# Full attention with 16-channel heads: row-maximum products in whole sets of four, started in another row group, and the projected keys, queries and values read out of PSUM by ScalarE

## The chip, the cores and the metric

The kernel runs on one core of one Trainium2 chip. The metric is the device time of one execution in microseconds (us). The change touches one of the six stages of the kernel, the second layer's cross attention, which takes about 1,240 us of the 8,617 us.

## The reference, cut to what matters

The whole kernel is a decoder of two layers on x of shape (4, 512, 256). The stage in question computes, for each of 4 batches, with 16 heads of 16 channels, over 1,601 context positions:

```
q = _split_heads(Q @ W_q.T + b_q)
k = _split_heads(K @ W_k.T + b_k)
v = _split_heads(V @ W_v.T + b_v)
scores = jnp.einsum('bhqd,bhkd->bhqk', q, k) / jnp.sqrt(jnp.float32(D_K))
probs = jax.nn.softmax(scores, axis=-1)
ctx = jnp.einsum('bhqk,bhkd->bhqd', probs, v)
...
return ctx @ W_o.T + b_o
```

Q is the layer-normalised x; K and V are both the context.

## The kernel before

A head of 16 channels is padded to 32 rows, so four heads (j = 0 to 3) fill the 128 rows of TensorE (PE), each in its own row group of 32. A **unit** is one batch and one group of four heads: 4 batches by 4 groups, 16 units. All matrix data is 32-bit.

For softmax a unit needs the largest score of every row before the exponentials. The scores are therefore computed twice:

- **Chunks** (maximum products): 64 per unit, one for each head j, query tile t of 128 and key block n of 400 or 401 columns. `chunk` on PE writes a bank of a ring of three PSUM banks (`fa_ring`, L1845); VectorE (DVE) reduces it to one maximum per row (L1753). `row_max`, `turn_less` and `shift` then fold the negated maximum into the queries `Qm`.
- **Scores** proper (L1866): keys by rows, 128 by 512 for each j, into four banks `fa_sps` of their own; ScalarE (ACT) takes the exponential of each (L1715); `output` multiplies with the values into `fa_pv` (L1877).

A unit has 13 **slots**, one for each 128 keys. In slot s PE issues the scores of slot s + 1, and between them chunks of the next unit (so the chunks of unit u + 1 run beside the scores of unit u), then what stands below, then `output` of slot s. 64 chunks are spread over slots 0 to 10: 5 or 6 in each. Chunk i has head `i % FJ`, so the head with which a slot's chunks begin changes from slot to slot: slots 0 to 10 begin with heads 0, 1, 3, 1, 3, 1, 2, 0, 2, 0, 2. The scores always begin with head 0.

**Pieces** are the projections of keys, queries and values of the next batch: 33 in each batch (4 of Q, 16 of K, of which 4 have only 65 columns, 13 of V). They go through the same ring. They are issued one in a slot in the units of groups 1, 2 and 3 of the first three batches (all 13 slots of groups 1 and 2, slots 0 to 6 of group 3); group 0 has none, and batch 3 has none. The first batch's pieces stand ahead of unit 0, with unit 0's chunks between them. DVE adds the bias while it copies a piece out (L1741 V, L1744 Q, L1747 K).

In slot 1 PE issues `add_up` (the sums of the softmax, into the ring) and DVE takes the reciprocal (L1770) and scales (L1772). In slots 4 and 5 of a new batch `out_product` follows for the batch before.

Every engine works its own list in order. All users of the ring take turns in one order written out by hand (`turn`); PE waits before a turn until the user three turns earlier has been read out (`await_bank`), and one semaphore, `ring_free`, counts every read-out, since DVE does them all. The core of PE's loop:

```python
for j in range(FJ):
    if nxt and nxt != (u + 1, 0):
        scores(*nxt, j)
    if j < len(ahead):
        chunk(u + 1, ahead[j])
for i in ahead[FJ:]:
    chunk(u + 1, i)
...
output(u, slot)
```

Of the kernel before, what the change touches and what calls it, by code (L numbers as in the profile page):

```python
# [1554 lines left out]
def lay_full_attention(a, rows, cols):  # L1555
# [10 lines left out]
    for j in range(FJ):  # L1566
# [4 lines left out]
        "fa_wv": rows(g("W_v").T), "fa_bv": g("b_v"),  # L1571
# [5 lines left out]
def full_attention(nc, c):  # L1577
# [7 lines left out]
    CHUNKS = FJ * TB * NKB  # L1585
# [3 lines left out]
    with Scope(nc, "fa") as s:  # L1589
# [4 lines left out]
        bv = s.sb("bv", [P, D])  # L1594
# [24 lines left out]
        ring_free = s.sem("ring_free")  # L1619
        top_ready = s.sem("top_ready")  # L1620
# [40 lines left out]
        turn = {}  # L1661

        def take(*use):
            turn[use] = len(turn)

        for n in range(len(PIECES)):
            take("piece", 0, n)
            for i in first_chunks(n - FIRST) if n >= FIRST else ():
                take("chunk", 0, i)
        take("less", 0)  # L1670
        for u, (b, g) in enumerate(UNITS):
            for slot in range(KT):
                for i in chunks_of(slot) if u < LAST_UNIT else ():
                    take("chunk", u + 1, i)
                if slot == LESS_SLOT and u < LAST_UNIT:
                    take("less", u + 1)
                if piece_of(u, slot) is not None:
                    take("piece", b + 1, piece_of(u, slot))
                if slot == SUMS_SLOT and u:
                    take("sums", u - 1)  # L1680
# [10 lines left out]
        def _(sp):  # L1691
            for dst, src in ((wq, "wq"), (wk, "wk"), (bqk, "bqk"), (wv, "wv"), (wo, "wo"), (sums, "sums")):
                sp.dma_start(dst[:], c.dram[f"fa_{src}"]).then_inc(loaded, 16)
            for dst, src in ((bv, "bv"), (bo, "bo")):
                sp.dma_start(dst[:], c.dram[f"fa_{src}"].partition_broadcast(P)).then_inc(loaded, 16)
# [6 lines left out]
        def _(pool):  # L1702
            nc.gpsimd.memset(less[:], 0.0).then_inc(made, 1)
            nc.gpsimd.memset(V[:, :, :, :, FD:], 1.0).then_inc(made, 1)
            pool.wait_ge(loaded, LOADS)
            nc.gpsimd.tensor_tensor(c.x[:], c.x[:], bo[:].unsqueeze(1).broadcast_to([P, NT, D]), ALU.add).then_inc(based, 1)

        @block.scalar
        def _(act):
# [6 lines left out]

            def take_output(u):
# [5 lines left out]
            for u in range(len(UNITS)):  # L1723
                for kt in range(KT):
                    exps(u, kt)
                    if kt == 0 and u:
                        take_output(u - 1)
            take_output(LAST_UNIT)

        @block.vector  # L1730
        def _(dve):
            def await_turn(*use):
                dve.wait_ge(ring_ready, turn[use] + 1)

            def piece(b, n):
                what, g, m = PIECES[n]
                await_turn("piece", b, n)
                src = bank("piece", b, n)
                if what == "V":
                    rows = keys(m)  # L1740
                    ins = nc.vector.tensor_tensor(V[0:rows, b % 2, m, :, 0:FD], src[0:rows, 0:D].rearrange("p (h d) -> p h d", d=FD),  # L1741
                                                  bv[0:rows, :].rearrange("p (h d) -> p h d", d=FD), ALU.add)
                elif what == "Q":
                    ins = nc.vector.tensor_scalar(Q[:, b % 2, g, :], src[:], bqk[:, 0, g:g + 1], None, ALU.add)  # L1744
                else:
                    k0, w = KEYS[m]
                    ins = nc.vector.tensor_scalar(K[:, b % 2, g, k0:k0 + w], src[:, 0:w], bqk[:, 1, g:g + 1], None, ALU.add)  # L1747
                ins.then_inc(ring_free, 1)
# [7 lines left out]
            def row_max(u):  # L1756
                dve.wait_ge(ring_free, turn["chunk", u, CHUNKS - 1] + 1)
# [5 lines left out]
            def shift(u):  # L1763
                b, g = UNITS[u]
                await_turn("less", u)
                nc.vector.tensor_tensor(Qm[:, u % 2, :], bank("less", u)[:], Q[:, b % 2, g, :], ALU.add).then_inc(ring_free, 1)

            def scale(u):
                await_turn("sums", u)
                nc.vector.reciprocal(share[:], bank("sums", u)[:]).then_inc(ring_free, 1)  # L1770
                dve.wait_ge(ring_free, turn["sums", u] + 1)
# [11 lines left out]
            for n in range(len(PIECES)):  # L1783
                piece(0, n)
                for i in first_chunks(n - FIRST) if n >= FIRST else ():
                    chunk(0, i)
# [3 lines left out]
            for u, (b, g) in enumerate(UNITS):  # L1790
                for slot in range(KT):
                    if u < LAST_UNIT:
                        for i in chunks_of(slot):
                            chunk(u + 1, i)
                        if slot == MAX_SLOTS - 1:
                            row_max(u + 1)
                        if slot == LESS_SLOT:
                            shift(u + 1)
                    if piece_of(u, slot) is not None:
                        piece(b + 1, piece_of(u, slot))  # L1800
# [9 lines left out]
        def _(pe):  # L1810
            def await_bank(*use):

                if turn[use] >= RING:
                    pe.wait_ge(ring_free, turn[use] - RING + 1)
# [21 lines left out]
            def chunk(u, i):  # L1836
# [4 lines left out]
                if i == 0:  # L1841
                    pe.wait_ge(ring_free, turn["piece", b, PIECES.index(("K", g, len(KEYS) - 1))] + 1)
# [13 lines left out]
            def scores(u, kt, j):  # L1856
# [4 lines left out]
                if kt == 0 and j == 0:  # L1861
                    pe.wait_ge(ring_free, turn["less", u] + 1)
# [6 lines left out]
            def output(u, kt):  # L1869

                b, g = UNITS[u]
                n = keys(kt)
                if kt == 0 and u:
# [25 lines left out]
            pe.wait_ge(made, MADE)  # L1899
            for n in range(len(PIECES)):  # L1900
# [1241 lines left out]
```

## Time and profile before

| | |
|---|---|
| median of 3 runs | 8619.73 us (8613.97 to 8625.38) |
| the profiled execution's own time | 8617.03 us |
| its span, first to last instruction | 8615.2 us |
| mean granted TensorE clock | 0.913 |
| the stage: first piece to last `out_product` | about 6720 to 7955 us of the span |
| PE, DVE, ACT busy over the whole span | 83%, 56%, 33% |

PE is the matmul stream and PEld the weight loads beside it. A 32-bit matmul shows as two instructions. In a timeline row the columns are the start, the length, the engine and line, the operation, what is written and read, how many instructions are merged, and in brackets the idle time before them with what ended it. "PEclk" is the clock that was granted, 1.00 being 2.4 GHz and 0.50 being 1.2 GHz.

### The profile page before, as it was taken

The numbers are of one execution on the slowest core, as the hardware profiler recorded it, in microseconds if no ns is written. First come the engines' busy times: TensorE is split into PE (matmuls) and PEld (weight loads), VectorE is DVE, ScalarE is ACT, GpSimd is POOL, SyncE is SP. The second block draws the span as 40 slices with busy tenths as digits, with TensorE's granted clock in tenths as the row PEclk, the third lists the DMA queues.
The fourth block names the chain that finished last, engine by engine and source line by source line (L and its number), as shares of the span: only waits on it lengthen the run. The fifth ranks groups of instructions, "written<-read, shape, count | busy, mean of one in ns | idle before, by whom it ended". The sixth has DMA issues, their size and how long they took to land. (4 is left out here: it accounts for less than half of the span.)

```text
span 8615.2 us, 102487 instructions
## 1 busy us (share of the span) xinstructions
PE 7109.9 (83%) x35402; PEld 4802.5 (56%) x35402; DVE 4861.0 (56%) x7898; ACT 2854.5 (33%) x5165; POOL 711.7 (8%) x695
## 2 busy tenths in 40 slices
PE   6887887887879888888888889956653899999799
PEld 4775766756757666666666744422222334333577
DVE  5656655656646666666666610058886555555621
ACT  3223222232224444444444411134441233334210
POOL 0111111111100000000000000023333000000000
PEclk8998998998989999999999999978886899999895
DMA  0000000000000000000000010000000000000110
GB/s 33 0 1 1 0 1 1 0 1 1 0 33 9 7 20 9 7 20 7 8 19 9 7 55 0 0 18 0 0 0 3 26 8 1 8 1 1 40 49 10
DMA packets 23873, 89.02 MB, mean 10 GB/s; under 512 B 5784, under 2 KB 9120, under 8 KB 18480
## 3 DMA queue, kind: packets, MB, share of 16 engines
q1 hardware_dynamic: 23456, 83.53, 2.8%
q8 instruction: 253, 4.15, 0.2%
q14 instruction: 164, 1.34, 0.1%
HBM read 81.43 MB, written 2.10 MB: 10 GB/s over the span
## 5 line engine op out<-in xcount | busy, mean ns | idle before, releaser
L1252 DVE TENSOR_TENSOR xa_PT<-xa_tps,xa_PT 128x512 fp32r<-128x512 f32 (+1 forms) x1024 | 555.3, 584 | 386.0 <-ACT xa_PT L1127 382.3
L1753 DVE TENSOR_REDUCE fa_part<-fa_ring 128x1 f32<-128x400 f32 (+1 forms) x1024 | 533.0, 569 | 330.2 <-PE fa_ring L1845 312.3
L1715 ACT ACTIVATE fa_prob<-fa_sps 128x512 f32<-128x512 f32 (+1 forms) x832 | 439.9, 601 | 782.8 <-PE fa_sps L1866 774.1
L635 DVE TENSOR_TENSOR gdn_XX<-gdn_XX,gdn_wps 128x512 f32<-128x512 f32 (+1 forms) x768 | 477.2, 640 | 367.8 <-PE gdn_wps L799 360.1
L496 ACT ACTIVATE gdn_Y<-gdn_yps 128x256 f32<-128x256 f32 x768 | 295.2, 384 | 1051.6 <-PE gdn_yps L784 1045.2
L1405 PE MATMUL xa_tps<-ident,xa_prob 128*128 128x128 f32 (+1 forms) x3328 | 501.4, 284 | 162.3 <-DVE xa_PT L1252 161.6
L1845 PE MATMUL fa_ring<-fa_K,fa_Q 32*128 32x400 f32 (+1 forms) x2048 | 586.6, 546 | 36.7 <-DVE fa_part L1753 23.5
L1405 PEld LDWEIGHTS xa_tps<-ident,xa_prob 128*128 128x128 f32 (+1 forms) x3328 | 393.1, 143 | 388.6 <-DVE xa_PT L1252 317.7
L1127 ACT ACTIVATE xa_PT<-xa_tps 128x512 fp32r<-128x512 f32 (+1 forms) x1024 | 471.2, 514 | 416.1 <-PE xa_tps L1405 415.9
L796 PE MATMUL gdn_wps<-gdn_Y,gdn_XX 128*128 128x128 f32 x3072 | 601.2, 287 | 2.9
L1240 DVE CUSTOM_DVE_ANT_0 xa_prob<-xa_sps,xa_mask 128x1604 f32<-128x1604 f32 x256 | 467.4, 1826 | 130.0 <-PE xa_sps L1387 123.4
L796 PEld LDWEIGHTS gdn_wps<-gdn_Y,gdn_XX 128*128 128x128 f32 x3072 | 472.9, 196 | 67.4 <-issue 35.9
L1115 ACT ACTIVATE xa_prob<-xa_prob,xa_neg 128x1604 f32<-128x1604 f32 x256 | 418.2, 1634 | 268.2 <-DVE xa_neg L1243 268.1
L799 PE MATMUL gdn_wps<-gdn_XX,gdn_Y 128*128 128x128 f32 x2560 | 503.5, 279 | 0.0
L1387 PE MATMUL xa_sps<-xa_K,xa_Q 128*128 128x402 f32 x2048 | 466.7, 372 | 29.6 <-issue 16.9
L1423 PE MATMUL xa_pv<-xa_PT,xa_V 128*128 128x256 f32 (+1 forms) x3328 | 453.4, 292 | 11.1 <-DVE xa_PT L1252 11.1
L2042 PE MATMUL ffn_mid<-ffn_hid,ffn_h 128*128 128x512 f32 x1024 | 441.5, 593 | 9.7 <-DVE ffn_hid L2008 6.3
L1423 PEld LDWEIGHTS xa_pv<-xa_PT,xa_V 128*128 128x128 f32 (+1 forms) x3328 | 415.9, 189 | 49.2 <-issue 28.8
L2361 DVE TENSOR_TENSOR_SCAN scan_h<-scan_dA,scan_dBx 128x2048 f32<-128x2048 f32 x64 | 407.8, 6372 | 26.4 <-POOL scan_dBx L2235 20.2
L1387 PEld LDWEIGHTS xa_sps<-xa_K,xa_Q 128*128 128x128 f32 x2048 | 382.7, 198 | 45.1 <-issue 36.0
L799 PEld LDWEIGHTS gdn_wps<-gdn_XX,gdn_Y 128*128 128x128 f32 x2560 | 398.5, 196 | 0.0
L1845 PEld LDWEIGHTS fa_ring<-fa_K,fa_Q 32*128 32x128 f32 x2048 | 245.9, 187 | 270.9 <-DVE fa_part L1753 222.2
(424 smaller groups left out, 12365.8 us busy)
## 6 DMA issues: line engine op xcount, KB each, us to landing
xa_wqk<-in_xa_wqk SPq DMA_DIRECT2D x64, 256.0 KB, 2.6
moe_own_w<-in_moe_w SPq DMA_DIRECT2D x14, 1024.0 KB
ffn_h<-in_ffn_h SPq DMA_DIRECT2D x2, 4096.0 KB, 27.5
xa_ctxT<-in_ctxT SPq DMA_DIRECT2D x4, 1601.0 KB
fa_ctxT<-in_ctxT SPq DMA_DIRECT2D x4, 1601.0 KB
xa_mask<-in_mask SPq DMA_DIRECT2D x4, 802.0 KB, 9.0
ffn_w<-in_ffn_w SPq DMA_DIRECT2D x3, 1024.0 KB, 18.1
x<-in_x SPq DMA_DIRECT2D x1, 2048.0 KB
```

The lines of the kernel that those rows point to most:

```text
L635: nc.vector.tensor_tensor(X[:, half, 0:n], X[:, half, 0:n], wps[half][:, 0:n], ALU.subtract).then_inc(X_ready, 1)
L796: last = nc.tensor.matmul(wps[half][:, 0, e, :], X[:, half, 1, e, :], Y[:, h, :], start=True, stop=True)
L799: last = nc.tensor.matmul(wps[half][:, 1, e, :], Y[:, h, :], X[:, half, 1, e, :], start=True, stop=True)
L1127: nc.scalar.activation(PT[0:n, u // 2 % NPT, 0, k0:k1, u % 2, :], turned_bank(u, g)[0:n, 0:k1 - k0, :], ACT.Copy).then_inc(t_hi, 1)
L1240: nc.vector.tensor_tensor_reduce(parts(prob[:, e, :]), sps[:, :, 0:SW], parts(mask[:, u % TB if masked else 0, :]), 1.0, -3.0e38, ALU.add, ...
L1252: nc.vector.tensor_tensor(PT[0:n, u // 2 % NPT, 1, k0:k1, u % 2, :], turned_bank(u, g)[0:n, 0:k1 - k0, :], PT[0:n, u // 2 % NPT, 0, k0:k1, ...
L1387: last = nc.tensor.matmul(sps[:, n, 0:SWW], Q[:, hh % 2, e, q * P:(q + 1) * P], k, start=(e == 0), stop=(e == 1))
L1405: last = nc.tensor.transpose(turned_bank(u, g)[0:n, kt - k0, :], prob[:, u % 2, kt * P:kt * P + n], c.ident[:])
L1423: nc.tensor.matmul(pv[0:MV, 0:2 * P], V[0:n, kt, hh].rearrange("p e d -> p (e d)"), PT[0:n, pair % NPT, part, kt].rearrange("p a q -> p (a ...
L1753: nc.vector.tensor_reduce(part[:, t, j, n:n + 1], bank("chunk", u, i)[:, 0:KB[n][1]], AX, ALU.max).then_inc(ring_free, 1)
L1845: nc.tensor.matmul(bank("chunk", u, i)[:, 0:w], Q[rows, b % 2, g, t * P:(t + 1) * P], K[rows, b % 2, g, k0:k0 + w], start=True, stop=True) ...
L2042: last = nc.tensor.matmul(mid[m % 2][:], w[n][:, k, m * P:(m + 1) * P], hid[e][:, k, :], start=(k == 0), stop=(k == MH - 1))
```

## The change

1. Chunks are dealt out in sets of four (`QUADS`, 16 to a unit): every slot from 0 to 10 has one set between the scores (`early`), and slots 2, 4, 6, 8 and 10 have a second one (`late`). `chunk_at` shifts the head by two, so every set begins with head 2 while the scores begin with head 0.
2. A late set comes after the slot's piece and before `output`. In slots without a late set `output` moves ahead of `add_up` and of `out_product`.
3. Pieces are read out by ScalarE (`piece` under `block.scalar`), in its list after the exponentials of the slot and before those of the next; a second semaphore, `piece_taken`, counts them, and `await_bank` picks the semaphore by who had the bank (`nth`).
4. ScalarE can't add a bias along the row to V, so the bias of V is folded into that of the output: GpSimd spreads it (`bv_wide`), PE multiplies it with the output weights into a first turn of the ring (`base`, eight matmul instructions of 256 columns) before the first piece, DVE adds that to `bo`, and GpSimd's addition of `bo` to x waits for it.

```diff
-            return range(CHUNKS * min(slot, MAX_SLOTS) // MAX_SLOTS, CHUNKS * min(slot + 1, MAX_SLOTS) // MAX_SLOTS)
+            first, last = (QUADS * min(n, MAX_SLOTS) // MAX_SLOTS * FJ for n in (slot, slot + 1))
+            return range(first, min(first + FJ, last)), range(first + FJ, last)
...
-            return i % FJ, i // FJ // NKB, i // FJ % NKB
+            return (i + FJ // 2) % FJ, i // FJ // NKB, i // FJ % NKB
...
+            nc.gpsimd.tensor_copy(bv_wide[:], bv[:].unsqueeze(2).broadcast_to([P, FG, P])).then_inc(spread_ready, 1)
+            pool.wait_ge(ring_free, nth["base",])
             nc.gpsimd.tensor_tensor(c.x[:], c.x[:], bo[:].unsqueeze(1).broadcast_to([P, NT, D]), ALU.add).then_inc(based, 1)
...
+            def piece(b, n):
+                what, g, m = PIECES[n]
+                act.wait_ge(ring_ready, turn["piece", b, n] + 1)
+                src = bank("piece", b, n)
+                if what == "V":
+                    rows = keys(m)
+                    ins = nc.scalar.activation(V[0:rows, b % 2, m, :, 0:FD], src[0:rows, 0:D].rearrange("p (h d) -> p h d", d=FD), ACT.Copy)
+                elif what == "Q":
+                    ins = nc.scalar.activation(Q[:, b % 2, g, :], src[:], ACT.Identity, bias=bqk[:, 0, g:g + 1])
+                else:
+                    k0, w = KEYS[m]
+                    ins = nc.scalar.activation(K[:, b % 2, g, k0:k0 + w], src[:, 0:w], ACT.Identity, bias=bqk[:, 1, g:g + 1])
+                ins.then_inc(piece_taken, 1)
...
                 for kt in range(KT):
                     exps(u, kt)
                     if kt == 0 and u:
                         take_output(u - 1)
+                    if piece_of(u, kt) is not None:
+                        piece(b + 1, piece_of(u, kt))
...
             def await_bank(*use):
 
                 if turn[use] >= RING:
-                    pe.wait_ge(ring_free, turn[use] - RING + 1)
+                    before = uses[turn[use] - RING]
+                    pe.wait_ge(piece_taken if before[0] == "piece" else ring_free, nth[before])
...
+            pe.wait_ge(spread_ready, 1)
+            for g in range(FG):
+                last = nc.tensor.matmul(bank("base")[:, 0:D], bv_wide[:, g, :], wo[:, g, :], start=(g == 0), stop=(g == FG - 1))
+            last.then_inc(ring_ready, 1)
...
                     for j in range(FJ):
-                        if nxt and nxt != (u + 1, 0):
-                            scores(*nxt, j)
-                        if j < len(ahead):
-                            chunk(u + 1, ahead[j])
-                    for i in ahead[FJ:]:
-                        chunk(u + 1, i)
+                        if slot + 1 < KT:
+                            scores(u, slot + 1, j)
+                        if j < len(early):
+                            chunk(u + 1, early[j])
                     if slot == LESS_SLOT and u < LAST_UNIT:
                         turn_less(u + 1)
                     if piece_of(u, slot) is not None:
                         piece(b + 1, piece_of(u, slot))
-                    if nxt == (u + 1, 0):
+                    if slot + 1 == KT and u < LAST_UNIT:
                         for j in range(FJ):
-                            scores(*nxt, j)
+                            scores(u + 1, 0, j)
+                    if not late:
+                        output(u, slot)
+                    for i in late:
+                        chunk(u + 1, i)
                     if slot == SUMS_SLOT and u:
                         add_up(u - 1)
                     if slot in OUT_SLOTS and u and ends(u - 1):
                         out_product(b - 1, OUT_SLOTS.index(slot))
-                    output(u, slot)
+                    if late:
+                        output(u, slot)
```

## Rows read from the trace of the kernel before

**Rows 1.** Busy time (instructions) of PE, PEld, DVE, ACT, POOL, then PEclk: units 0 and 14.

```profile
6804.00:6866.00 62.00, 59.81 (x332) 23.82 (x328) 34.18 (x67) 26.45 (x51) 0.00 (x0) 0.90 0.01 4
...
7836.00:7902.00 66.00, 63.25 (x348) 23.45 (x344) 38.65 (x70) 28.44 (x55) 0.00 (x0) 0.92 0.00 1
```

**Rows 2.** Timeline of ACT in unit 0, the exponentials of slots 3 to 12.

```profile
6821.80 2.06 ACT L1715 ACTIVATE fa_prob<-fa_sps 128x512 f32<-128x512 f32 x4 [2.58 <-PE fa_sps L1866]
6826.59 2.26 ACT L1715 ACTIVATE fa_prob<-fa_sps 128x512 f32<-128x512 f32 x4 [2.72 <-PE fa_sps L1866]
...
6840.57 2.06 ACT L1715 ACTIVATE fa_prob<-fa_sps 128x512 f32<-128x512 f32 x4 [2.10 <-PE fa_sps L1866]
6845.21 2.29 ACT L1715 ACTIVATE fa_prob<-fa_sps 128x512 f32<-128x512 f32 x4 [2.58 <-PE fa_sps L1866]
6850.48 2.06 ACT L1715 ACTIVATE fa_prob<-fa_sps 128x512 f32<-128x512 f32 x4 [2.98 <-PE fa_sps L1866]
...
6864.98 2.05 ACT L1715 ACTIVATE fa_prob<-fa_sps 65x512 f32<-65x512 f32 x4 [2.52 <-PE fa_sps L1866]
```

**Rows 3.** Timeline of one slot with six chunks, and the next one's start.

```profile
7809.27 0.18 PEld L1866 LDWEIGHTS fa_sps<-fa_Qm,fa_K 32*128 32x128 f32 x1 [0.85 <-issue]
...
7810.47 3.14 DVE L1753 TENSOR_REDUCE fa_part<-fa_ring 128x1 f32<-128x401 f32 x6 [1.50 <-PE fa_ring L1845]
...
7811.10 0.29 PEld L1845 LDWEIGHTS fa_ring<-fa_K,fa_Q 32*128 32x128 f32 x2 [0.68 <-DVE fa_part L1753]
...
7812.06 0.29 PEld L1845 LDWEIGHTS fa_ring<-fa_K,fa_Q 32*128 32x128 f32 x2 [0.19 <-DVE fa_part L1753]
7812.93 0.13 PEld L1877 LDWEIGHTS fa_pv<-fa_prob,fa_V 128*17 128x17 f32 x8 [0.57 <-ACT fa_prob L1715]
...
7813.91 0.33 PEld L1866 LDWEIGHTS fa_sps<-fa_Qm,fa_K 32*128 32x128 f32 x8 [0.85 <-issue]
...
7815.74 3.14 DVE L1753 TENSOR_REDUCE fa_part<-fa_ring 128x1 f32<-128x400 f32 x6 [2.13 <-PE fa_ring L1845]
```

**Rows 4.** Timeline of ACT, slots 0 and 1 of the fifth unit.

```profile
7105.78 2.29 ACT L1715 ACTIVATE fa_prob<-fa_sps 128x512 f32<-128x512 f32 x4
...
7116.47 1.57 ACT L1715 ACTIVATE fa_prob<-fa_sps 128x512 f32<-128x512 f32 x3 [3.64 <-PE fa_sps L1866]
```

**Rows 5.** Timeline around the reciprocal, with a piece of Q after the chunks.

```profile
7045.27 3.36 DVE L1770 RECIPROCAL fa_share<-fa_ring 128x512 f32<-128x512 f32 x1 [0.63 <-PE fa_ring L1885]
...
7046.14 0.18 PEld L1866 LDWEIGHTS fa_sps<-fa_Qm,fa_K 32*128 32x128 f32 x1 [0.85 <-issue]
...
7048.68 0.18 PEld L1845 LDWEIGHTS fa_ring<-fa_K,fa_Q 32*128 32x128 f32 x1 [1.39 <-DVE fa_share L1770]
...
7049.89 0.29 PEld L1845 LDWEIGHTS fa_ring<-fa_K,fa_Q 32*128 32x128 f32 x2 [0.91 <-DVE fa_part L1753]
...
7051.72 0.30 PEld L1828 LDWEIGHTS fa_ring<-xnT,fa_wq 128*128 128x128 f32 x2 [0.57 <-DVE fa_part L1753]
...
7053.63 0.13 PEld L1877 LDWEIGHTS fa_pv<-fa_prob,fa_V 128*17 128x17 f32 x8 [0.76 <-issue]
```

**Rows 6.** Waits in the stage: total us, times, longest us.

```profile
PEld fa_sps L1866 <- ACT fa_prob L1715: 28.7, 48, 2.2
```

**Rows 7.** Groups by line on ACT: line, shapes, count, busy us, mean ns, idle.

```profile
L496 ACT ACTIVATE gdn_Y<-gdn_yps 128x256 f32<-128x256 f32 x768 | 295.2, 384 | 1051.6 <-PE gdn_yps L784 1045.2
...
L1105 ACT ACTIVATE xa_Q<-xa_proj,xa_bqk 128x512 fp32r<-128x512 f32 x64 | 43.8, 685 | 51.7 <-PE xa_proj L1369 51.6
```

**Rows 8.** Timeline of the start of the stage.

```profile
6716.12 8.82 POOL L1706 TENSOR_TENSOR x<-x,fa_bo 128x4096 f32<-128x4096 f32 x1 [7.82 <-DMA fa_bo<-in_fa_bo]
...
6720.05 3.75 PE L1828 MATMUL fa_ring<-xnT,fa_wq 128*128 128x512 f32 x4 [14.87 <-DMA fa_ctxT<-in_ctxT]
...
6724.44 0.34 PEld L1832 LDWEIGHTS fa_ring<-fa_ctxT,fa_wk 128*128 128x128 f32 x1 [0.52 <-issue]
6725.02 0.19 PEld L1832 LDWEIGHTS fa_ring<-fa_ctxT,fa_wk 128*128 128x128 f32 x1 [0.24 <-issue]
```

More of the change, by code:

```diff
@@ L1659, in ends @@
             return UNITS[u][1] == FG - 1
-        turn = {}
+        turn, uses, nth = {}, [], {}
+        counts = {True: 0, False: 0}
         def take(*use):
             turn[use] = len(turn)
+            uses.append(use)
+            counts[use[0] == "piece"] += 1
+            nth[use] = counts[use[0] == "piece"]
+        take("base")
         for n in range(len(PIECES)):
@@ L1672, in full_attention @@
             for slot in range(KT):
-                for i in chunks_of(slot) if u < LAST_UNIT else ():
+                early, late = chunks_of(slot) if u < LAST_UNIT else ((), ())
+                for i in early:
                     take("chunk", u + 1, i)
@@ L1678, in full_attention @@
                     take("piece", b + 1, piece_of(u, slot))
+                for i in late:
+                    take("chunk", u + 1, i)
                 if slot == SUMS_SLOT and u:
@@ L1721, in take_output @@
                 nc.scalar.activation(raw[:], pv[:], ACT.Copy).then_inc(raw_ready, 1)
-            for u in range(len(UNITS)):
+            act.wait_ge(loaded, LOADS)
+            act.wait_ge(made, MADE)
+            for n in range(len(PIECES)):
+                piece(0, n)
+            for u, (b, g) in enumerate(UNITS):
                 for kt in range(KT):
@@ L1782, in _ @@
             dve.wait_ge(made, MADE)
[L1783 to L1786, printed above, removed]
+            dve.wait_ge(ring_ready, turn["base",] + 1)
+            nc.vector.tensor_tensor(bo[:], bank("base")[:, 0:D], bo[:], ALU.add).then_inc(ring_free, 1)
+            for i in range(CHUNKS):
+                chunk(0, i)
             row_max(0)
@@ L1791, in _ @@
                 for slot in range(KT):
-                    if u < LAST_UNIT:
-                        for i in chunks_of(slot):
-                            chunk(u + 1, i)
[L1795 to L1800, printed above, removed]
+                    early, late = chunks_of(slot) if u < LAST_UNIT else ((), ())
+                    for i in early:
+                        chunk(u + 1, i)
+                    if slot == LESS_SLOT and u < LAST_UNIT:
+                        shift(u + 1)
+                    for i in late:
+                        chunk(u + 1, i)
+                    if slot == MAX_SLOTS - 1 and u < LAST_UNIT:
+                        row_max(u + 1)
                     if slot == SUMS_SLOT and u:
@@ L1841, in chunk @@
                 if i == 0:
-                    pe.wait_ge(ring_free, turn["piece", b, PIECES.index(("K", g, len(KEYS) - 1))] + 1)
+                    pe.wait_ge(piece_taken, nth["piece", b, PIECES.index(("K", g, len(KEYS) - 1))])
                 await_bank("chunk", u, i)
@@ L1861, in scores @@
                 if kt == 0 and j == 0:
-                    pe.wait_ge(ring_free, turn["less", u] + 1)
+                    pe.wait_ge(ring_free, nth["less", u])
                 if at >= FJ:
@@ L1872, in output @@
                 n = keys(kt)
+                if kt == 0 and g == 0:
+                    pe.wait_ge(piece_taken, nth["piece", b, PIECES.index(("V", 0, KT - 1))])
                 if kt == 0 and u:
```

40 lines of the change are left out of this document (15 added, 25 removed).

## The prediction

> **What bounds the stage now.** I read the busy times by window first, one window to a unit [rows 1]. PE is busy for 96% of every unit (59.81 of 62, 63.25 of 66), DVE for 55 to 60%, ACT for some 43% in these two; nothing is loaded from outside that anyone waits for. So the stage goes at the pace of PE's list, and PE's list is in order: what counts is how long each slot holds it.
>
> Next, ACT's timeline, because each slot's exponentials start 1.16 us after PE starts the slot's scores, so they mark the slots [rows 2]. Slots 3 to 10 of unit 0 take 6864.98 - 6826.59 = 38.39 us together. With six chunks a slot that begins with head 3 takes 6826.59 - 6821.80 = 4.79, one with head 2 takes 6845.21 - 6840.57 = 4.64, and one with head 0, the head with which the scores begin too, 6850.48 - 6845.21 = 5.27.
>
> Then one slot from inside [rows 3]. Counted from its first score at 7809.27: first reduce +1.20, weights of the fourth chunk +1.83, of the sixth +2.79, `output` +3.66, next slot +4.64. The fourth chunk waits for the first one's bank, and so on: a chunk is reduced 0.98 after its weights start (7812.06 against the last of six reduces, 7810.47 + 3.14 - 0.57), and its bank is free 0.57 + 0.06 later, so three chunks turn round in 1.61, some 0.5 each. After the last chunk's weights PE needs 0.87 until it can go on, and `output` takes 0.98. In the slot that begins with head 0 the first reduce comes 7815.74 - 7813.91 = 1.83 after the start, not 1.20.
>
> **Part 1, sets of four from head 2.** A slot with one set: the fourth chunk's weights at +1.83, +0.87 = 2.70, `output` 0.98: 3.68 us. A slot with two sets and no piece: fourth chunk reduced at +2.81, so the seventh starts at +3.44 and the eighth, likewise, at +3.92; +0.87 + 0.98 = 5.77. The eleven slots before, without the sums: slots 0 and 1 take 7116.47 - 7105.78 = 10.69 [rows 4], of which `add_up` is 1.06 (an `output` is moved, not lengthened, by it), slot 2 is 4.79, slots 3 to 10 are 38.39: 52.81. After: 6 x 3.68 + 5 x 5.77 = 50.93. That is 1.9 us a unit, nearly all of it from the three slots that began with head 0 (3 x 0.63). The number of chunks is the same, and a set that is cut off early only brings the next slot forward.
>
> The row already shows the new pairing, since slots 6, 8 and 10 begin with head 2: their first reduce still comes at +1.20, 0.04 after the first exponential. By the Trainium skill (TensorE: Matmul & The Clock Gate, "What overlaps and what doesn't") matmuls end strictly in program order, so a chunk issued behind a score can't end ahead of it, in whatever row group. The trace agrees by that +1.20; if it were not so, the first reduce could come near +0.98, and the eleven sets of fifteen units would save 0.22 each, 36 us more.
>
> **Part 2, `output` ahead of `add_up`.** Before, the reciprocal starts at 7045.27, while PE is in `output`, and slot 2 begins at 7046.14. The third chunk needs the bank of the sums and waits until 7048.68 (+2.54), with the fourth score behind it; the fourth starts at +3.75, PE goes on at 7051.72 (+5.58), and with `output` slot 2 holds PE for 6.56 [rows 5]. After, `add_up` is the last thing of slot 1, so the reciprocal starts 0.10 after slot 2 begins: third chunk at 0.10 + 3.36 + 0.02 = +3.48; DVE scales until +4.15, so the fourth starts at +4.78, the seventh at +6.39, the eighth at +6.87; + 0.87 + 0.98 = 8.72. With slot 1 at 3.68 + 1.06 = 4.74 the unit's eleven slots are 5 x 3.68 + 4.74 + 8.72 + 4 x 5.77 = 54.94, against 10.69 + 6.56 + 38.39 = 55.64 before. So of the 1.9 gained, 1.2 goes back: 0.7 is left. Sum of the units with chunks beside them: unit 0 (no sums) -1.9, the other fourteen -0.7 each: **-11.7 us**.
>
> **Part 3, pieces by ScalarE.** What DVE gives up (0.42 for a V, 0.75 for a Q or K) lies in its idle time before the slot's first reduce, so it is worth nothing. What ACT takes on is small too: nearest rows 0.38 for 128x256 and 0.69 for 128x512 with a bias [rows 7], 99 pieces in the steady part, ACT at 43% at most. What matters is its place in ACT's list: the exponentials of the next slot now wait for the piece. Let P be the end of the piece's matmuls. In a slot with one set PE does `output` and is at the next scores at P + 0.98. ACT ends the piece at P + 0.5 (V) or P + 0.85 (Q, K) and its four exponentials (0.49 apart) free the score banks at P + 1.16 to 2.63, or 1.45 to 2.90. PE's list has each score between chunks, so the last score starts some 1.7 or 1.95 into the slot where the fourth chunk would start at 1.83 anyway. I take 0.1 us for V (and the 65-column K) and 0.3 for Q and K; bounds are 0 (the fourth chunk hides it) and the whole piece, 0.38 and 0.69. Slot 1 is covered by `add_up`. There are 7 wide and 6 narrow such slots in a batch: 2.7 us; slot 12 of group 1 another 0.3.
>
> In a slot with two sets the piece now cuts the run of eight. The second set finds two banks free at P; its third chunk has the piece's bank, read out at P + 0.55 to 0.85; its fourth waits for the first: 0.98 + 0.57 + 0.06 = P + 1.61, and PE goes on at P + 2.48. Uncut it would be 4.79 + piece - (2.70 + piece) = 2.09 for these four. So 0.39 for each of 13 such slots: 5.1 us a batch. Bounds: 0 and 0.7. The pieces themselves cost PE what they did, 7053.63 - 7051.72 = 1.91 for a Q or K [rows 5]. Over three batches: 3 x (2.7 + 0.3 + 5.1) = **+24.3 us**.
>
> **Part 4, the bias.** The first piece waits for the context until 6720.05. `bo` has landed by 6716.12; GpSimd spreads 512 elements (an eighth of 8.82, 1.1 us), so `base` starts near 6717.3 and its eight instructions of 256 columns at half clock take some 3.4 us, to 6720.8: 0.7 late. But PE runs at half clock from 6720.0 to about 6725.0 (weight loads 0.34, then 0.19) [rows 8], and if those five microseconds at half clock start 2.7 us earlier, 1.35 comes back. In the rest of the startup PE's list sets the pace and DVE's share is hidden. **-0.5 us**, bounds -2 and +1. The later addition of `bo` to x on GpSimd has 80 us to end in.
>
> **Clock.** The granted clock is 0.90 to 1.00 in the units. A unit loses (1 - clock) x its length, from 6.2 us (unit 0) and 5.3 (unit 14) [rows 1] to 0 in the four units of group 3; summed over fifteen such windows 34 us. In several the low clock follows the stall behind the reciprocal, during which PE has nothing for 1.5 us. That stall is now 1 us longer and comes in every unit, so I expect a low stretch (1.6 us) where there was none or less: **+8 us**, bounds -34 (all gone) and +25.
>
> **Sum.** -11.7 + 24.3 - 0.5 + 8 = +20.1. The profiled execution took 8617.0, so 8637; the median of the runs is 2.7 above it: 8640 us.
>
> **Rivals.**
> - *Faster: the clock holds.* The slots with one set are 3.68 us with no DVE wait beyond the fourth chunk, so PE's work is denser between stalls. If the low stretches disappear, -34 takes the place of +8: 8620 - 11.7 + 24.3 - 0.5 - 34 = 8598. It decides from -30 on, so nearly all must go. Against it: PE's longest stall grows.
> - *Faster: read-out by two engines.* PE's weight loads wait for DVE before the fourth and later chunks of every slot. If DVE's pace, not the turn-round of three banks, set these waits, taking 52 x 0.42, 16 x 0.75 and 64 x 0.64 us from it would show: up to 22 + 12 + 41 = 75 us in all, and at three fifths of that 8620 + 20 - 45 = 8595. Against it: those read-outs fall where DVE is idle. The Trainium skill (TensorEngine Tiling (Array Packing), "PSUM Bottleneck") says to read PSUM out with both engines once tiling has sped up the matmuls. By that rule the change would gain; the rows say DVE has room.
> - *No measurable change.* The waits for exponentials are hidden and the clock stays as it is: -11.7 + 3 x 5.1 (the cut runs only) = +3.6, 8623; with the 8 of the clock, 8632.
> - *Clearly slower: ACT becomes the chain.* In a run of slots with one set or two, piece, four exponentials, scores and the next piece hang on each other: 0.1 + 0.69 + 2.07 + 0.05 + 1.0 + 1.91 = 5.8 against 2.70 + 1.91 + 0.98 = 5.6 for a slot with one set and a K. If each of the 99 pieces costs its upper bound (48 x 0.69 + 51 x 0.38 = 52.5 us for the 24.3 counted) the time is 8640 + 28 = 8668. It decides from 0.5 us a piece.
>
> **Chances.** My own sum 45%, its own range 8628 to 8658; no measurable change 23%; the clock holds 10%; two engines 10%; ACT as the chain 12%. A difference of 0.2% (17 us) is what a measurement of this kernel can tell from none. My sum is only just beyond it: about a fifth of that case falls inside, most of "no change" too. Together: faster 20%, within 0.2% 32%, slower 48%. For the range I take in both outer cases to their prices but leave their far sides: 8598 to 8670.
>
> **What the profile after would show.** Slots with one set and no piece 3.7 us apart, with two 5.8; first reduce +1.20 in all of them; the reciprocal starting with slot 2's first score and that slot at 8.7; exponentials after a piece starting at P + 0.5 to 0.9 and PE's weight loads of scores waiting for ACT more than the 28.7 us of before [rows 6]; the second set after a piece 2.5 long; no unit at clock 1.00. Wrong would be: second sets that run at more than two chunks at once, which would make the order pay, or units of batch 3, which have no pieces, that differ by more than 1 us from before.

## The result, and the profile after

| | before | after |
|---|---|---|
| median | 8619.93 us (5 runs, 8613.97 to 8626.68) | 8668.87 us (5 runs, 8660.9 to 8674.14) |
| profiled execution, its span | 8617.03, 8615.2 us | 8673.85, 8672.1 us |
| the stage, between the two table loads that bracket it | 1265.8 us | 1314.8 us |

The ratio is 1.0055, 95% interval 1.0041 to 1.007: slower by 49 us where 20 were forecast. In the profiled executions the stage grew by 49.0 us; the other 8 us between the two lie ahead of it, in code that is the same.

Inside the stage, measured from one `fa_raw` to the next, the part ahead of unit 0 is 1.7 us shorter, unit 0 is 1.7 longer, units 1 to 14 are 50.0 longer, and unit 15 with the tail is 1.1 shorter. To see what the clock took I add up (1 - clock) x length over the fifteen lengths that begin at the first `fa_raw`, which are units 1 to 15: 27.3 us before and 74.1 after. I call this sum the loss. Unit 0 stands outside it and loses 6.2 us before (62 x 0.10) and 10.9 after (64 x 0.17).

The windows of after that answer [rows 1], with a batch 3 unit behind them (columns as there):

```profile
6811.00:6875.00 64.00, 63.16 (x332) 25.07 (x328) 34.54 (x67) 26.24 (x51) 0.00 (x0) 0.83 0.01 2
7825.00:7893.00 68.00, 66.13 (x343) 26.05 (x342) 38.59 (x69) 27.49 (x53) 0.00 (x0) 0.85 0.00 1
7893.00:7962.00 69.00, 67.12 (x350) 26.55 (x344) 38.59 (x69) 27.74 (x55) 0.00 (x0) 0.85 0.00 1
```

DVE and ACT have as much room as before; what fell is the clock, from 0.90 and 0.92 to 0.83 and 0.85, in units that have no pieces at all. ACT's timeline in the unit at 7825, the exponentials of slots 5 to 12, shows where:

```profile
7852.33 2.06 ACT L1729 ACTIVATE fa_prob<-fa_sps 128x512 f32<-128x512 f32 x4 [1.48 <-PE fa_sps L1887]
7859.53 2.07 ACT L1729 ACTIVATE fa_prob<-fa_sps 128x512 f32<-128x512 f32 x4 [5.13 <-PE fa_sps L1887]
7863.21 2.06 ACT L1729 ACTIVATE fa_prob<-fa_sps 128x512 f32<-128x512 f32 x4 [1.61 <-PE fa_sps L1887]
7870.57 2.06 ACT L1729 ACTIVATE fa_prob<-fa_sps 128x512 f32<-128x512 f32 x4 [5.29 <-PE fa_sps L1887]
7874.25 2.06 ACT L1729 ACTIVATE fa_prob<-fa_sps 128x512 f32<-128x512 f32 x4 [1.61 <-PE fa_sps L1887]
7880.01 2.06 ACT L1729 ACTIVATE fa_prob<-fa_sps 128x512 f32<-128x512 f32 x4 [3.70 <-PE fa_sps L1887]
7883.69 2.06 ACT L1729 ACTIVATE fa_prob<-fa_sps 128x512 f32<-128x512 f32 x4 [1.61 <-PE fa_sps L1887]
7890.99 2.05 ACT L1729 ACTIVATE fa_prob<-fa_sps 65x512 f32<-65x512 f32 x4 [5.24 <-PE fa_sps L1887]
```

Slots with one set take 3.68 us (7863.21 - 7859.53), as forecast. Of the four with two sets one takes the forecast 5.76 (7880.01 - 7874.25), the other three 7.20, 7.36 and 7.30. The windows of 2 us over the second of the long ones:

```profile
7862.00:7864.00 2.00, 1.98 (x19) 1.06 (x16) 0.74 (x2) 0.79 (x2) 0.00 (x0) 1.00 0.00 0
7864.00:7866.00 2.00, 2.00 (x9) 1.08 (x9) 1.94 (x5) 1.28 (x3) 0.00 (x0) 1.00 0.00 0
7866.00:7868.00 2.00, 2.00 (x12) 0.42 (x10) 1.55 (x3) 0.00 (x0) 0.00 (x0) 0.65 0.00 0
7868.00:7870.00 2.00, 2.00 (x16) 0.84 (x11) 0.00 (x0) 0.00 (x0) 0.00 (x0) 0.50 0.00 0
7870.00:7872.00 2.00, 1.97 (x14) 0.79 (x8) 1.39 (x3) 1.43 (x3) 0.00 (x0) 0.99 0.00 0
```

and rows of its timeline:

```profile
7863.26 4.42 DVE L1772 TENSOR_REDUCE fa_part<-fa_ring 128x1 f32<-128x401 f32 x8 [1.50 <-PE fa_ring L1866]
...
7864.37 0.29 PEld L1866 LDWEIGHTS fa_ring<-fa_K,fa_Q 32*128 32x128 f32 x2 [0.19 <-DVE fa_part L1772]
...
7865.49 0.29 PEld L1866 LDWEIGHTS fa_ring<-fa_K,fa_Q 32*128 32x128 f32 x2 [0.35 <-DVE fa_part L1772]
7865.97 0.29 PEld L1866 LDWEIGHTS fa_ring<-fa_K,fa_Q 32*128 32x128 f32 x2 [0.19 <-DVE fa_part L1772]
7867.00 0.15 PEld L1900 LDWEIGHTS fa_pv<-fa_prob,fa_V 128*17 128x17 f32 x8 [0.74 <-issue]
7867.00 1.91 PE L1900 MATMUL fa_pv<-fa_prob,fa_V 128*17 128x512 f32 x8
7868.84 0.28 PEld L1887 LDWEIGHTS fa_sps<-fa_Qm,fa_K 32*128 32x128 f32 x1 [1.69 <-issue]
```

Eight reduces run without a gap (4.42 us); PE, at full clock, starts each chunk from the fourth on when a bank comes free. Behind the eighth the clock is 1.2 GHz for some 3 us: `output` holds PE 1.84 instead of 0.98, the scores behind it the rest. The slot is 7.36 - 5.76 = 1.60 longer, and by (1 - clock) x length the three windows lose 0.70 + 1.00 + 0.02 = 1.72: a lost microsecond is 0.93 us of time here.

The reciprocal, after, which answers [rows 5]:

```profile
7835.42 3.36 DVE L1790 RECIPROCAL fa_share<-fa_ring 128x512 f32<-128x512 f32 x1 [1.47 <-PE fa_ring L1908]
...
7838.83 0.18 PEld L1866 LDWEIGHTS fa_ring<-fa_K,fa_Q 32*128 32x128 f32 x1 [2.55 <-DVE fa_share L1790]
...
7840.05 1.45 PEld L1866 LDWEIGHTS fa_ring<-fa_K,fa_Q 32*128 32x128 f32 x6 [0.91 <-DVE fa_part L1772]
...
7844.52 1.91 PE L1900 MATMUL fa_pv<-fa_prob,fa_V 128*17 128x512 f32 x8
...
7846.36 0.28 PEld L1887 LDWEIGHTS fa_sps<-fa_Qm,fa_K 32*128 32x128 f32 x1 [1.69 <-issue]
```

Slot 2 begins at 7835.32; the third chunk starts at +3.51 (forecast 3.48), the fourth at +4.73 (4.78). The rest was to end at 8.72 and ends at 11.04, its `output` at half clock. This is where most of the new loss stands. The table gives the loss of units 1 to 14 in slots 2 and 3, beside and behind the reciprocal, and in slots 4 to 10, each slot taken from its first weight load of `fa_sps` to that of the next; the last two rows are experiments described below.

| | slots 2 and 3 | slots 4 to 10 |
|---|---|---|
| before | 20.5 us | 8.5 us |
| after | 57.3 | 16.0 |
| `sums_first` (the shorter stall of before, runs of eight as after) | 22.2 | 16.2 |
| `set_after_output` (the longer stall as after, no run of eight) | 54.6 | 0.0 |

These sums take the clock as it is and not rounded to 0.01, so they add up to 1 or 2 us more than the 27.3 and 74.1. Of the rise, 37 us stand in slots 2 and 3, and 35 of them go again when only the longer stall is taken back; 7.5 net stand in slots 4 to 10. Slot 2 of unit 5 in these four kernels, in this order:

```profile
7188.77:7197.24 8.47, 7.64 (x36) 2.67 (x32) 6.91 (x9) 2.17 (x4) 0.00 (x0) 1.00 0.00 0
7206.86:7220.93 14.07, 12.11 (x37) 4.00 (x36) 8.18 (x10) 3.35 (x7) 0.00 (x0) 0.76 0.00 0
7194.75:7204.73 9.98, 9.16 (x40) 2.96 (x36) 7.31 (x10) 3.54 (x7) 0.00 (x0) 1.00 0.00 0
7193.33:7206.56 13.23, 10.85 (x36) 3.12 (x35) 6.70 (x8) 3.34 (x7) 0.00 (x0) 0.74 0.00 0
```

ACT's groups, which answer [rows 7], and two rows of the waits in the stage, the first of which answers [rows 6]:

```profile
L1742 ACT ACTIVATE fa_K<-fa_ring,fa_bqk 128x512 f32<-128x512 f32 x64 | 38.0, 595 | 214.2 <-PE fa_ring L1853 214.2
L1737 ACT ACTIVATE fa_V<-fa_ring 128x256 f32<-128x256 f32 (+1 forms) x52 | 20.0, 385 | 166.8 <-PE fa_ring L1846 166.8
L1739 ACT ACTIVATE fa_Q<-fa_ring,fa_bqk 128x512 f32<-128x512 f32 x16 | 11.0, 687 | 91.3 <-PE fa_ring L1849 91.3
```

```profile
PEld fa_sps L1887 <- ACT fa_prob L1729: 139.3, 263, 2.2
...
PEld fa_ring L1866 <- DVE fa_share L1790: 35.7, 14, 2.6
```

Reading a piece takes what [rows 7] said, 385 and 687 ns. PE's wait for exponentials rose from 28.7 us in 48 waits to 139.3 in 263, but most of that is probably time in which it would have waited for a bank next: its waits for `fa_part` before chunks fell from 213 to 152 us, and `sets_only`, which has only 56 us of these waits, is no faster. The cut second set behind a V, from its first weights to `output`:

```profile
6937.19 0.30 PEld L1866 LDWEIGHTS fa_ring<-fa_K,fa_Q 32*128 32x128 f32 x4 [0.33 <-DVE fa_part L1772]
...
6938.80 0.29 PEld L1866 LDWEIGHTS fa_ring<-fa_K,fa_Q 32*128 32x128 f32 x2 [0.77 <-DVE fa_part L1772]
6939.66 0.13 PEld L1900 LDWEIGHTS fa_pv<-fa_prob,fa_V 128*17 128x17 f32 x8 [0.57 <-ACT fa_prob L1729]
```

2.47 us, the fourth chunk at +1.61, as forecast (2.48, 1.61). And the start of the stage, which answers [rows 8]:

```profile
6725.28 3.75 PE L1925 MATMUL fa_ring<-fa_wo,fa_bv_wide 128*128 128x256 f32 x8 [11.45 <-POOL fa_bv_wide L1718]
6728.41 0.75 PEld L1849 LDWEIGHTS fa_ring<-xnT,fa_wq 128*128 128x128 f32 x2
...
6730.26 0.19 PEld L1849 LDWEIGHTS fa_ring<-xnT,fa_wq 128*128 128x128 f32 x1 [0.24 <-issue]
```

The stage starts 8.67 us later in this execution, so before's first piece would stand at 6728.72; here it has its weights at 6728.41, and the half clock is over at 6730.26 instead of 6733.69 (6725.02 + 8.67).

### The profile page after: what moved, and what is told of

Read it like the earlier page. It is cut to its first block and busy times, and to the rows that moved or that the text cites. A ratio compares the mean times of both kernels' runs of the same rounds, so it can differ in the third digit from the quotient of the medians.

```text
span 8672.1 us, 102523 instructions
## 1 busy us (share of the span) xinstructions
PE 7164.7 (83%) x35410; PEld 4828.1 (56%) x35410; DVE 4794.8 (55%) x7767; ACT 2903.1 (33%) x5297; POOL 711.3 (8%) x696
## 5 line engine op out<-in xcount | busy, mean ns | idle before, releaser
L1866 PE MATMUL fa_ring<-fa_K,fa_Q 32*128 32x400 f32 (+1 forms) x2048 | 691.1, 579 | 30.5 <-DVE fa_share L1790 24.1
L1887 PE MATMUL fa_sps<-fa_Qm,fa_K 32*128 32x512 f32 (+1 forms) x1664 | 436.7, 664 | 7.4 <-ACT fa_prob L1729 6.6
L2390 DVE TENSOR_TENSOR_SCAN scan_h<-scan_dA,scan_dBx 128x2048 f32<-128x2048 f32 x64 | 407.6, 6370 | 26.4 <-POOL scan_dBx L2264 20.2
L1866 PEld LDWEIGHTS fa_ring<-fa_K,fa_Q 32*128 32x128 f32 x2048 | 274.7, 196 | 239.3 <-DVE fa_part L1772 161.4
```

Source lines behind the costliest of these rows:

```text
L1866: nc.tensor.matmul(bank("chunk", u, i)[:, 0:w], Q[rows, b % 2, g, t * P:(t + 1) * P], K[rows, b % 2, g, k0:k0 + w], start=True, stop=True) ...
```

## The experiments

Theory A, formed on these rows: a long run of chunks paced by the banks, and the longer stall at the reciprocal, lower the clock, and that is what the forecast lacked. Rival B: the read-out by ScalarE costs more than counted and is the loss. Each result is a median with its ratio to before and that ratio's 95% interval; the loss is that of the one profiled execution, so a time and a loss can come from different executions.

**One part at a time.** `sets_only` is the kernel after with `piece` moved back from ScalarE's list to VectorE's.

```diff
-                ins = nc.scalar.activation(Q[:, b % 2, g, :], src[:], ACT.Identity, bias=bqk[:, 0, g:g + 1])
+                ins = nc.vector.tensor_scalar(Q[:, b % 2, g, :], src[:], bqk[:, 0, g:g + 1], None, ALU.add)
```

> The changed kernel with the pieces read out by VectorE again (the order of PE's list, the sets of four and the bias product stay). In the changed kernel unit windows lose some 85 us to a granted clock under 1.00, against 34 before, and the low stretches stand behind the runs of eight chunks. Theory A (the runs of eight lower the clock, ScalarE is nearly innocent): the waits for exponentials after a piece go (9 us), the rest stays, so about 8655 us, and the low stretches in the units without pieces stay where they are. Rival B (pieces on ScalarE are the cost): most of the 49 us goes, about 8620 us.

Measured: 8673.25, ratio 1.0059 [1.0047, 1.0071], loss 97.6. Parts 1, 2 and 4 by themselves cost 52 us where -12.2 were counted. Rival B falls. Theory A's 8655 was missed too, by 18 us: it did not expect the loss to rise, and it is 23.5 us over after's. The rise is mostly in slots 4 to 10 (34.8 against 16.0). In the six units in which every slot has a piece, so that a piece stands between the two sets, after loses nothing there; `sets_only` loses 12.0, in slots 4 and 5 of three of them, and why is not known.

`act_only` is the kernel after with before's dealing and `output` last.

```diff
-            first, last = (QUADS * min(n, MAX_SLOTS) // MAX_SLOTS * FJ for n in (slot, slot + 1))
-            return range(first, min(first + FJ, last)), range(first + FJ, last)
+            return range(CHUNKS * min(slot, MAX_SLOTS) // MAX_SLOTS, CHUNKS * min(slot + 1, MAX_SLOTS) // MAX_SLOTS), ()
...
-            return (i + FJ // 2) % FJ, i // FJ // NKB, i // FJ % NKB
+            return i % FJ, i // FJ // NKB, i // FJ % NKB
```

> The changed kernel with the chunks dealt out as before (5 or 6 in a slot, beginning with changing heads) and output last in each slot, so only the read-out by ScalarE and the bias product are new. Theory A: no run of eight, so the clock is as before; what is left is the wait for exponentials behind a piece, up to 0.3 us for 33 pieces in three batches, 8625 to 8645 us. Rival B: 8660 us or more.

Measured: 8635.48, ratio 1.0016 [1.0007, 1.0024], loss 25.0. ScalarE's read-out, with the bias product, costs 14 us (6 to 21 by the interval) and leaves the clock alone. Beside sets it costs nothing on balance (after is 4 us under `sets_only`, within what the two intervals allow), because there the loss is 23.5 us smaller with it.

**Where `output` stands.** `sums_first` is the kernel after with `output` last in every slot.

```diff
-                    if not late:
-                        output(u, slot)
...
-                    if late:
-                        output(u, slot)
+                    output(u, slot)
```

> The changed kernel with output behind add_up and out_product again, in every slot. My sum: the reciprocal starts 1 us earlier against slot 2, 1.2 us in each of 14 units, so 17 us less than the changed kernel, 8652 us; if the shorter stall also spares a low stretch in part of the units, down to 8640. Rival: the reciprocal's stall has nothing to do with PE's pace, no difference, 8669 us.

Measured: 8633.09, ratio 1.0018 [1.0008, 1.0028], loss 42.0: 36 us under after, more than expected. The loss fell by 32 us, all of it in slots 2 and 3 (57.3 to 22.2), while the runs of eight in slots 4 to 10 lose what they did (16.0 and 16.2). So the longer stall is what brought most of the low clock. The fifteen lengths are 41.2 us shorter together: if the stall itself is the 17 counted, 24 are the clock, and if each lost microsecond costs 0.93, 30 are the clock and 11 the stall.

`set_after_output` is the kernel after with `output` ahead of the second set, so that no eight chunks follow each other.

```diff
-                    if not late:
-                        output(u, slot)
+                    output(u, slot)
                     for i in late:
                         chunk(u + 1, i)
...
-                    if late:
-                        output(u, slot)
```

> The changed kernel with the second set behind output instead of ahead of it, so no run is longer than four between outputs, and the next slot's scores follow the second set directly. By turn-round a slot with two sets takes about the same, 5.4 to 5.8 us. Theory A: the windows of the units without pieces rise from 0.85 to 0.93 or more, 30 to 45 us less than the changed kernel, 8625 to 8640. Rival C (VectorE-paced sets lower the clock wherever they stand): no change of the clock, 8660 to 8670.

Measured: 8619.27, ratio 0.9998 [0.9989, 1.0007], loss 53.9: 50 us under after. About 19 of them are the clock (20.2 x 0.93). With no run of eight, slots 4 to 10 lose 0.0 us; what is left stands behind the stall, 54.6 in slots 2 and 3. At full clock two slots together take 9.22 (ACT's timeline, 7829.84 to 7839.06) instead of 9.44, because the banks come free under `output`: five pairs in fifteen units are 17 more. In the two profiled executions the fifteen lengths differ by 40.8 us, so some 5 of these are not placed. That the medians differ by 50 and these executions, 8673.85 and 8631.34 us, by 42.5 is the spread of the runs.

**Where the chunks begin.** `head2` is the kernel before with each slot's chunks dealt to heads 2, 3, 0, 1 and then one or two others, in its 5 and 6; `head0` is the kernel after with sets that begin with head 0.

```diff
+        tails = [(2,), (2, 1), (2, 1), (3, 1), (3, 1), (3,), (0, 1), (2, 0), (2, 0), (3, 0), (3, 0)]
+        heads = [j for slot in range(MAX_SLOTS) for j in (2, 3, 0, 1) + tails[slot]]
+        deal = [(j, heads[:i].count(j)) for i, j in enumerate(heads)]
...
-            return i % FJ, i // FJ // NKB, i // FJ % NKB
+            j, m = deal[i]
+            return j, m // NKB, m % NKB
```

> The kernel before with only the heads of its chunks dealt anew: every slot begins with heads 2, 3, 0, 1, then one or two others; 5 or 6 a slot as before. By the rows of before a slot with six from head 2 takes 4.64 us, from head 0 5.27, heads 1 and 3 4.8: 2.7 us less in each of 15 units, 41 us less than before, 8579 us, if the clock stays as before. Rival (denser chunk runs lower the clock again, so the gain is given back): 8600 to 8620 us.

Measured: 8568.79, ratio 0.9938 [0.9925, 0.9951], loss 20.8: 51 us faster than before, with nothing of parts 2 to 4, where 41 were counted at an unchanged clock. The 8.5 us that before lost in slots 4 to 10 are gone (0.0); the 20.5 in slots 2 and 3 are still there.

> The changed kernel with chunks that begin with head 0, as the scores do. The rows of before price a start with head 0 at 0.63 us a slot: 11 slots, 15 units, 104 us more than the changed kernel, 8770. Rival (the pairing hardly matters, since matmuls end in program order anyway): under 8690.

Measured: 8752.82, ratio 1.0158 [1.0143, 1.0174], loss 59.7: 84 us over after. In its unit 13 a slot with one set takes 4.31 and one with two 6.39, each 0.63 over after's, so the term per slot is as counted; the clock holds in these slots, and the two that follow each other there take 10.70, less than after's 11.04 with a low stretch. The loss is 14.4 us smaller than after's, some 13 us of time, which is most of what is missing from the 104.

**How long a run.** In these four VectorE reads everything, `output` is last and every slot begins with heads 2, 3, 0, 1, as in `head2`; the number of chunks in each slot differs, and with it the heads of the fifth and later ones. The edit of `light_slot2`:

```diff
+    COUNTS = [6, 6, 2, 7, 6, 6, 6, 7, 6, 6, 6] + [0, 0]
...
-            return range(CHUNKS * min(slot, MAX_SLOTS) // MAX_SLOTS, CHUNKS * min(slot + 1, MAX_SLOTS) // MAX_SLOTS)
+            return range(sum(COUNTS[:slot]), sum(COUNTS[:slot + 1]))
```

> head2 with two chunks in slot 2, beside the reciprocal, and the others dealt over the remaining slots (6 each, 7 in slots 3 and 7). Only two chunks need no bank that waits for the reciprocal, so PE should have no stall there: slot 2 takes about 2.65 us in place of 6.56, four more chunks elsewhere cost 2.0: 1.9 us less in each of 14 units, 27 us less than head2, 8542 us, and 8520 if the low clock behind the reciprocal goes too. Rival: the stall only moves to slot 3, whose chunks wait for VectorE, no gain, 8569.

Measured: 8545.71, ratio 0.9912 [0.9897, 0.9927], loss 4.4: 23 us under `head2`, the fastest kernel of the study. With two chunks beside the reciprocal nothing waits for the bank of the sums, and slot 2 holds PE for 2.73 us (ACT's timeline, 7787.25 to 7789.98); twelve of the fifteen unit windows are at clock 1.00 and three at 0.98. The low clock behind the reciprocal did go, but the 8520 expected for that case was not reached: the fifteen lengths are 28.4 us shorter than `head2`'s, of which 16.3 are loss, so the slots themselves gave some 13 where 27 were counted.

`runs_5_7`:

```diff
+    COUNTS = [5, 7, 5, 7, 5, 7, 5, 7, 5, 7, 4] + [0, 0]
```

> head2 with runs of 5 and 7 chunks by turns (4 in slot 10) in place of 6 in nearly every slot; all begin with head 2, all else equal. By the turn-round of banks 0.85 us more a unit, 13 us: 8582. Theory A (the clock falls behind long runs in which PE waits for banks): runs of seven show low stretches too, five a unit at most, 8600 to 8650. Rival C (the clock falls because of the mode of the runs as such or the order of the second set, not their length): 8582.

Measured: 8584.21, ratio 0.9961 [0.9947, 0.9975], loss 23.4: 15 us over `head2`, about what the banks' turn-round was counted at (0.85 us in each of 15 units, 13). Runs of seven hardly lower the clock: the loss is 2.6 us over `head2`'s, and slots 4 to 10 lose 1.7 us in fourteen units. In three units, though, a low stretch now begins in slot 1, which has seven chunks.

`runs_4_8`:

```diff
+    COUNTS = [4, 8, 4, 8, 4, 8, 4, 8, 4, 8, 4] + [0, 0]
```

> The kernel before with head2's order of heads, VectorE reading everything and output last, but 4 and 8 chunks alternately (4 in slot 10) where runs_5_7 had 5 and 7. By the turn-round of the banks the two cost the same: a slot takes 3.68, 4.16, 5.29 and 5.77 us with 4, 5, 7 and 8 chunks, so five pairs and the last are 50.93 us in either. Theory A (a run of eight chunks ahead of output lowers the clock, a run of seven does not): the clock falls in many of the five such slots of a unit; from 75 of them with a low stretch in a third to all, at 1.0 to 1.5 us each, 25 to 90 us over runs_5_7's 8584, so 8610 to 8670, and units whose loss by (1 - clock) x length sums to 50 or more, against 23. Rival: the eighth chunk does nothing by itself, and the low clock of the changed kernel came from output moved ahead or from its longer stall at the reciprocal: 8584 within 5, loss 20 to 30.

Measured: 8608.78 (11 runs), ratio 0.9986 [0.9977, 0.9995], loss 46.9. Moving one chunk from each slot of five to the slot of seven beside it, at the same sum by turn-round, costs 25 us (22 by the two ratios); the loss is 23.5 us more, and in slots 4 to 10 it is 21.7 against 1.7. Theory A's lower figures, 8610 us and a loss of 50, are both missed by a little; the rival's 8584 is far off.

`light_4_8`:

```diff
+    COUNTS = [8, 4, 2, 8, 4, 8, 4, 8, 4, 8, 6] + [0, 0]
```

> As light_slot2 (two chunks beside the reciprocal, so no stall there), but the other slots hold 8, 4, 8, 4 and so on instead of 6 and 7: five runs of eight. By the turn-round alone 5 x 5.77 + 4 x 3.68 + 4.64 = 48.21 us against 8 x 4.64 + 2 x 5.29 = 47.70, 0.5 a unit, 8 us: 8553. Theory A (runs of eight lower the clock by themselves): 8575 to 8640, and the loss by the clock over the units rises from 4 us to 30 or more. Rival (eight chunks lower it only in units where a stall at the reciprocal stands ahead of them): 8553 within 5, and the loss stays under 10.

Measured: 8586.26, ratio 0.9961 [0.9947, 0.9975], loss 36.3: 41 us over `light_slot2`, of which 8 are turn-round, and the loss rose by 31.9. There is no stall at the reciprocal in it. ACT's timeline of one unit shows the same two kinds of slots as after's:

```profile
7776.41 2.06 ACT L1722 ACTIVATE fa_prob<-fa_sps 128x512 f32<-128x512 f32 x4 [3.78 <-PE fa_sps L1873]
7780.09 2.06 ACT L1722 ACTIVATE fa_prob<-fa_sps 128x512 f32<-128x512 f32 x4 [1.61 <-PE fa_sps L1873]
7785.85 2.06 ACT L1722 ACTIVATE fa_prob<-fa_sps 128x512 f32<-128x512 f32 x4 [3.70 <-PE fa_sps L1873]
7789.53 2.06 ACT L1722 ACTIVATE fa_prob<-fa_sps 128x512 f32<-128x512 f32 x4 [1.61 <-PE fa_sps L1873]
7796.94 2.07 ACT L1722 ACTIVATE fa_prob<-fa_sps 128x512 f32<-128x512 f32 x4 [5.35 <-PE fa_sps L1873]
```

3.68, 5.76, 3.68, 7.41: the same eight chunks, with and without the low clock behind them. Its unit windows beside those of `light_slot2`, first `light_slot2`:

```profile
7719.32:7776.19 56.87, 56.72 (x346) 23.09 (x342) 37.94 (x69) 27.48 (x55) 0.00 (x0) 1.00 0.00 1
```

then `light_4_8`:

```profile
7754.74:7815.54 60.80, 60.62 (x346) 24.32 (x342) 38.28 (x69) 27.47 (x54) 0.00 (x0) 0.94 0.00 1
```

The same instructions, 3.93 us longer: 0.5 of turn-round and a loss of 60.80 x 0.06 = 3.6, which is 3.4 of time at 0.93.

## Why the prediction was right, and where its size was off

It said slower, most likely by 20 us, and it is slower by 49. The mechanisms of the slot were right; the term that was mis-sized is the clock, put at +8 with a bound of +25. Its loss rose by 74.1 - 27.3 = 46.8 us, and by 4.7 more in unit 0. What that is in time is known only roughly. A lost microsecond cost 0.93 in the slot above, 0.91 in `sets_only` (52 + 12.2 = 64 for 70.3), 0.88 in the fifteen lengths of `runs_4_8` against `runs_5_7` (20.8 for 23.5), and 0.74 in after's unit of 68.22 us against before's of 63.74, if parts 1 and 2 gave there what was forecast. So the clock is some 38 to 48 of the 49 us.

That the time lies inside the stated range of 8598 to 8670 is luck. It is above my own sum's range, which ended at 8658, and the last 12 us were taken in for ACT as the chain, which did not come about.

- **Part 1.** Slots of 3.68 and 5.76 and the first reduce at +1.20 came as forecast. The chunks don't end ahead of the scores: [rows 3] read rightly. Its gain is real: `head2`, which takes the gain and leaves the sets, is 51 us faster. The sum for the sets was missing the price of a run of eight: about 16 us of loss in slots 4 to 10, 8.5 of which only take the place of what before lost in these slots.
- **Part 2.** The stall came as worked out (+3.51, +4.73), in every unit. What followed was read too small: a low stretch did come behind it in all fourteen units, where before had one in nine, and `output` runs at half clock too. With the slot behind it that is 37 us more loss, against the 8 us that the sum gave the clock.
- **Part 3.** The cut run took 2.47. The 38 to 48 us of clock leave 1 to 11 of the stage's 49 for parts 1 to 4, where -11.7 + 24.3 - 0.5 = 12 were forecast. So the read-out by ScalarE cost 13 to 23 if the other parts came as forecast, at most about the 24 that were counted. `act_only` has 14 (6 to 21), in slots where no run is cut; how it splits into waits for exponentials and cut runs is not borne out.
- **Part 4.** -0.5 forecast; the part ahead of unit 0 is 1.7 shorter, and the half clock at its start is over 3.4 us earlier.
- **The clock.** I tied its low stretches to the stall behind the reciprocal, and priced one more short stretch a unit. The place was right: slots 2 and 3 lose 20.5 us before, against 8.5 in slots 4 to 10, and 57.3 against 16.0 after. The step that failed is the price of that stall, 8 us where `sums_first` shows 24 to 30. A second source was left out, and the rows of before had it. Three of its windows of 2 us:

```profile
7890.00:7892.00 2.00, 1.68 (x6) 0.88 (x6) 1.94 (x5) 1.31 (x3) 0.00 (x0) 1.00 0.00 0
7892.00:7894.00 2.00, 2.00 (x12) 0.17 (x11) 0.83 (x2) 0.00 (x0) 0.00 (x0) 0.52 0.03 8
7894.00:7896.00 2.00, 2.00 (x17) 1.40 (x14) 0.07 (x1) 0.12 (x1) 0.00 (x0) 0.62 0.00 0
```

and a row of the timeline ahead of them:

```profile
7890.32 0.29 PEld L1845 LDWEIGHTS fa_ring<-fa_K,fa_Q 32*128 32x128 f32 x2 [1.28 <-DVE fa_part L1753]
```

No reciprocal is near. What stands ahead is a slot of six chunks that begins with head 0, in which PE's weight loads waited 1.28 us for the first reduce: a low stretch can also follow waits inside a slot. That was so in four units of before, behind slots 7 and 9, which begin with head 0, and in none of `head2`.
- **The rivals.** The clock did not hold, it fell; two engines at the read-out gained nothing (`act_only` +14); ACT did not become the chain, though 8668 us was its time: it has the number of the result and not its cause, as `sets_only` shows, at 8673 with VectorE reading the pieces. No measurable change is out by the interval, which ends at 1.0041.

The forecast's own sign that something was wrong, units of batch 3 that differ by more than 1 us, came true: 68.22 and 68.21 against 63.74 and 65.63, with no piece in them. That batch is the place to look first.

One rule was there to be weighed and was not. The Trainium skill (TensorE: Matmul & The Clock Gate, "A second HAM failure mode: psum-queue depth-cycling") tells of a kernel whose PE pauses briefly between groups while it cycles through PSUM banks, often enough that the clock swings between its two levels. The trace agrees in kind: gaps of 0.19 to 0.35 us between the weight loads of the last chunks of a run of eight, then a granted clock of 0.65 and 0.50 in the next two windows.

**What stays open.** Why a run of eight is followed by the low clock in some slots (three of the four above) and not in all, and why a run of seven hardly ever is; why a stall that is 1 us longer lowers the clock in every unit; and how the stage's 49 us divide between the clock and parts 1 to 4 more closely than above.

## What to carry to other kernels

Deal work that PE issues under the pace of a few PSUM banks in even, short runs, and keep it away from the slot in which the vector engine holds a bank for long: 6 to a slot with 2 beside the reciprocal (8546 us) beat sets of 4 and 8 by 41 us with the same instructions. Begin such work in a row group other than that of the matmul ahead of it: dealt out so, the kernel before gained 0.6%. A stall costs more than its own length: the one at the reciprocal became 1 us longer, and the loss behind it rose from 20.5 to 57.3 us over fourteen units. And when a trace of before shows low clock, find what stands ahead of each such stretch before you price it: a change of order can multiply it.

## What the runs showed of the hardware that was not expected

- When PE's third chunk waits for the bank of the sums until +3.5 us into slot 2 and not +2.5, the loss in slots 2 and 3 of fourteen units is 57.3 us and not 22.2 (after, `sums_first`).
- The granted clock fell to 1.2 GHz for some 3 us though PE shows as busy for 1.98 and 2.00 of 2.00 us in the two windows ahead. What stood ahead was eight products of 32 rows by 401 columns, of which the last five waited for a bank. With runs of at most seven the loss was 23.4 us, with runs of eight 46.9 (`runs_5_7`, `runs_4_8`), and where nothing else stalls 4.4 and 36.3 (`light_slot2`, `light_4_8`).
- Most of the low clock of the kernel before and of `head2` could be removed: from 20.8 us to 4.4 by leaving PE nothing that waits behind the reciprocal (3.36 us for 128 by 512).
- A matmul that begins in the row group of the one ahead comes out 0.63 us later, and every slot is longer by just that (4.31 against 3.68, 6.39 against 5.76).
